# A four-layer cross-attention block on one core: another wait for v's copy, a term behind the relu, the relu in one pass with its bias folded into bf2

## The reference

```python
def _attention(x, src, dist, bias, ...):
    q = einsum('bfd,dnh->bfnh', x, Wq) * H ** (-0.5)
    k = einsum('btd,dnh->btnh', src, Wk);  v = einsum('btd,dnh->btnh', src, Wv)
    hbias = relu(dist[..., None] @ Wth + bth)          # 32 terms
    qs_bias = (hbias @ Wto + bto)[..., 0]
    w = softmax(einsum('btnh,bfnh->bnft', k, q) + bias + qs_bias[:, None])
    return einsum('bfnh,nhd->bfd', einsum('bnft,btnh->bfnh', w, v), Wo)

for i in range(4):
    x = x + _attention(_norm(x), ctx, dist, bias, Wq[i], Wk[i], Wv[i], Wo[i], ...)
    y = relu(_norm(x) @ Wf1[i] + bf1[i]) @ Wf2[i] + bf2[i]
    x = x + y
```

## Time and profile before

| | |
|---|---|
| median of 3 runs | 1341.23 us (1339.73 to 1343.92) |
| profiled execution | 1341.62 us, span 1339.6 us |
| TensorE matmul busy | 1208.2 us, 90% of the span |
| TensorE weight load | 991.7 us, 74% |
| VectorE | 1113.0 us, 83% |
| ScalarE | 1058.4 us, 79% |
| GpSimd | 719.8 us, 54% |
| DMA | 26.67 MB, 20 GB/s on average |

### The profile page before, as it was taken

The page is one execution under the profiler, slowest core; times in us unless marked ns, Lnnn a source line. Parts: engine busy times, 40 slices in busy tenths (PEclk is TensorE's granted clock), DMA queues, the critical chain, the costliest instruction groups (busy, mean ns, idle before and its releaser), DMA issues. The chain is left out here.

```text
span 1339.6 us, 36553 instructions
## 1 busy us (share of the span) xinstructions
PE 1208.2 (90%) x11184; PEld 991.7 (74%) x11184; DVE 1113.0 (83%) x4800; ACT 1058.4 (79%) x3353; POOL 719.8 (54%) x828
## 2 busy tenths in 40 slices
PE   2699999999999999999999999999999999789997
PEld 1577777777787777777777777877777777666665
DVE  4888888888888888888888888888888887579997
ACT  4688888888888888888888787878887865578896
POOL 3666666666666666656666665666666643211110
PEclk9899999999999999999999999999999999899999
DMA  6000000011100000011000000110000000000000
GB/s 189 17 1 17 2 18 1 17 33 34 35 17 2 17 2 17 2 57 43 10 9 10 10 2 18 49 43 9 18 1 25 2 2 4 1 10 14 14 16 9
DMA packets 32320, 26.67 MB, mean 20 GB/s; under 512 B 6648, under 2 KB 27008, under 8 KB 32128
## 3 DMA queue, kind: packets, MB, share of 16 engines
q1 hardware_dynamic: 32128, 24.35, 6.3%
HBM read 23.29 MB, written 1.05 MB: 18 GB/s over the span
## 5 line engine op out<-in xcount | busy, mean ns | idle before, releaser
L768 ACT ACTIVATE prob<-score,nmax 128x128 f32<-128x128 f32 x1024 | 397.1, 392 | 95.6 <-DVE nmax L963 93.9
L1367 POOL TENSOR_TENSOR prob<-prob,rinv 128x512 f32<-128x512 f32 x256 | 266.6, 1041 | 377.7 <-DVE rinv L971 377.0
L751 ACT ACTIVATE relu_z<-dist_g,cst_all 128x512 f32<-128x512 f32 x386 | 295.4, 805 | 12.5 <-DMA dist_g<-in_fside_BxSxS 10.1
L916 DVE SCALAR_TENSOR_TENSOR M<-relu_z,cst_all,M 128x512 f32<-128x512 f32 x370 | 277.7, 751 | 7.1 <-ACT relu_z L751 3.3
L963 DVE CUSTOM_DVE_ANT_0 score<-L,bias 128x128 f32<-128x128 f32 x1024 | 232.7, 283 | 2.0 <-PE L L485 0.9
L768 ACT ACTIVATION_READ_ACCUMULATOR prob<-score,nmax 128x1 f32 x1024 | 196.1, 191 | 0.0
L630 PEld LDWEIGHTS M<-wo,oT 128*128 128x128 f32 x1024 | 119.1, 191 | 66.7 <-ACT oT L780 66.6
L495 PE MATMUL T<-ident,prob 128*128 128x128 f32 x1024 | 161.3, 280 | 0.5 <-POOL prob L1367 0.5
L485 PE MATMUL L<-kT,qT 64*128 64x128 f32 x2048 | 149.7, 286 | 1.4 <-DVE nmax L963 1.4
L509 PE MATMUL O<-probT,v 128*64 128x128 f32 x2048 | 140.1, 278 | 8.8 <-issue 7.3
L630 PE MATMUL M<-wo,oT 128*128 128x128 f32 x1024 | 131.3, 281 | 15.0 <-ACT oT L780 15.0
(11 more groups left out here) (134 smaller groups left out, 2174.2 us busy)
## 6 DMA issues: line engine op xcount, KB each, us to landing
dist_g<-in_fside_BxSxS SPq DMA_DIRECT2D x16, 256.0 KB, 2.8
mask_g<-in_mask_Bx1x1xS_ff SPq DMA_DIRECT2D x16, 256.0 KB, 3.1
wk<-in_L_xattn_Wk SPq DMA_DIRECT2D x4, 512.0 KB, 3.5
wv<-in_L_xattn_Wv SPq DMA_DIRECT2D x4, 512.0 KB, 3.5
wq<-in_L_xattn_Wq SPq DMA_DIRECT2D x4, 512.0 KB, 3.9
wo<-in_L_xattn_Wo SPq DMA_DIRECT2D x4, 512.0 KB, 4.2
wf<-in_L_xattn_Wf SPq DMA_DIRECT2D x8, 256.0 KB, 2.8
xr<-in_x SPq DMA_DIRECT2D x16, 64.0 KB, 1.9
```

The costliest lines, as they stand in the source:

```text
L751: nc.scalar.activation(relu_z[:, z_slot(g, k), :], dist_g[:, :, :], ACT.Relu, bias=cst(g, C_BTH + k), scale=cst(g, C_WTH + k)).then_inc(z_ ...
L768: last = nc.scalar.activation(prob[:, c, m, :], score[:, c, m, :], ACT.Exp, bias=nmax[:, c, m:m + 1], scale=-1.0, accum_out=rsum[:, c, m:m ...
L916: vec.scalar_tensor_tensor(out=bias_acc[:, :], in0=relu_z[:, z_slot(g, k), :], scalar=weight, in1=bias_acc[:, :], op0=ALU.mult, op1=ALU.ad ...
L1367: gp.tensor_tensor(prob[:, c, :, :], prob[:, c, :, :], rinv[:, c, :].rearrange("p (m o) -> p m o", o=1).broadcast_to([P, 4, P]), ALU.mult) ...
```

## The change

Four edits, which share their semaphores.

1. ScalarE's copy of the first half of v waits for P V of octet 0 of the unit before last to be written (`after(g, i - 1, 2, 0)`), where it waited for octet 1 (`after(g, i - 1, 2, 1)`). The half that is overwritten is read by octet 0 alone.
2. On VectorE `terms(g, i, 0)` moves from ahead of the h2T copy to behind the relu.
3. The relu becomes one pass of 128x512: max(M1, -bf1) in place of max(M1 + bf1, 0). These differ by bf1, which is constant over positions.
4. The missing bf1 Wf2 is made once a layer and added to bf2: GpSimd writes -bf1 (128x4) and bf1 spread over 128 columns (128x512), TensorE multiplies it by Wf2 (four matmuls into T0), VectorE adds the result to bf2b. This is done in the first step for layer 0, and for the others in the second step of the last group of the layer before (GpSimd's part a step earlier). wf2, bf1c and bf2b get two buffers, and are loaded at the second group of the layer before.

```diff
+        def fold_layer(g, i):
+            if (g, i) == (0, 0):
+                return 0
+            if i == 1 and g % GROUPS_PER_LAYER == GROUPS_PER_LAYER - 1 and g < GROUPS - 1:
+                return g // GROUPS_PER_LAYER + 1
+            return None
@@ TensorE
+            def fold(g, i, l):
+                pe.wait_ge(w_f2, l * 16 + 16)
+                pe.wait_ge(fold_rep, 2 * l + 2)
+                pe.wait_ge(pT_even, after(g, i, 2, 0))
+                for c in range(FILT // P):
+                    last = mm(T[0][:, 0:P], bf1_rep[:, c, :], wf2[:, l % 2, c, :], start=c == 0, stop=c == FILT // P - 1)
+                last.then_inc(fold_done, 1)
...
+                folds = [] if i < 0 else [l for l in range(LAYERS) if (4 * g + i - 1) in ((0,) if l == 0 else (16 * l - 3,))]
+                for l in folds:
+                    pe.wait_ge(fold_kept, l + 1)
                 if prev:
                     turn(g, i - 1, 2)
...
                     queries(g, i + 1, 1)
+                if fold_layer(g, i) is not None:
+                    fold(g, i, fold_layer(g, i))
                 if cur:
                     apply(g, i, 0)
@@ ScalarE
                     act.wait_ge(v_done, after(g, i + 1, 2, 0))
-                    wait(act, pv_done, after(g, i - 1, 2, 1))
+                    wait(act, pv_done, after(g, i - 1, 2, 0))
@@ VectorE
                     inverse(g, i - 1, 3)
-                if i < GROUP:
-                    terms(g, i, 0)
...
-                    for c in range(FILT // P):
...
-                        last = vec.tensor_scalar(hid[:, i % 2, c, :], M1[:, c * P:(c + 1) * P], bf1c[:, c:c + 1], 0.0, ALU.add, ALU.max)
-                    last.then_inc(hid_kept, 1)
...
+                    vec.tensor_tensor(hid[:, i % 2, :, :], M1[:, :].rearrange("p (c t) -> p c t", c=FILT // P),
+                                      nbf1[:, l % 2, :].rearrange("p (c o) -> p c o", o=1).broadcast_to([P, FILT // P, P]),
+                                      ALU.max).then_inc(hid_kept, 1)
+                if i < GROUP:
+                    terms(g, i, 0)
...
+                if fold_layer(g, i) is not None:
+                    l = fold_layer(g, i)
+                    dve.wait_ge(fold_done, l + 1)
+                    dve.wait_ge(w_b2, l * 16 + 16)
+                    vec.tensor_tensor(bf2b[:, l % 2, :], T[0][:, 0:P], bf2b[:, l % 2, :], ALU.add).then_inc(fold_kept, 1)
@@ GpSimd
+                if fold_layer(g, i + 1) is not None:
+                    l = fold_layer(g, i + 1)
+                    pool.wait_ge(w_b1, l * 16 + 16)
+                    wait(pool, hid_kept, BATCHES * (l - 1))
+                    gp.tensor_scalar(nbf1[:, l % 2, :], bf1c[:, l % 2, :], -1.0, None, ALU.mult).then_inc(fold_rep, 1)
+                    wait(pool, fold_done, l)
+                    gp.tensor_copy(bf1_rep[:, :, :], bf1c[:, l % 2, :].rearrange("p (c o) -> p c o", o=1).broadcast_to(
+                        [P, FILT // P, P])).then_inc(fold_rep, 1)
                 if prev or there(g, i + 2):
                     root_pair(g, i)
```

More of the change, by code:

```diff
@@ L149, in block_program @@
         wf1 = sb("wf1", [P, FILT])
-        wf2 = sb("wf2", [P, FILT // P, P])
-        bf1c = sb("bf1c", [P, FILT // P])
-        bf2b = sb("bf2b", [P, P])
+        wf2 = sb("wf2", [P, 2, FILT // P, P])
+        bf1c = sb("bf1c", [P, 2, FILT // P])
+        nbf1 = sb("nbf1", [P, 2, FILT // P])
+        bf1_rep = sb("bf1_rep", [P, FILT // P, P])
+        bf2b = sb("bf2b", [P, 2, P])
         dist_g = sb("dist_g", [P, GROUP, P])
@@ L252, in block_program @@
         f1_done, hid_kept, f2_done = sem("f1_done"), sem("hid_kept"), sem("f2_done")
+        fold_rep, fold_done, fold_kept = [sem("fold_" + n) for n in ("rep", "done", "kept")]
         f_consts, f_in, f_gate_in, tanh_done = sem("f_consts"), sem("f_in"), sem("f_gate_in"), sem("tanh_done")
@@ L350, in load_f2 @@
             def load_f2(l):
-                sp.dma_start(wf2[:, :, :], Wf2[bass.ds(l, 1), :, :].rearrange("l (c p) d -> p (l c) d", p=P)).then_inc(w_f2, 16)
+                sp.dma_start(wf2[:, l % 2, :, :], Wf2[bass.ds(l, 1), :, :].rearrange("l (c p) d -> p (l c) d", p=P)).then_inc(w_f2, 16)
             def load_b1(l):
-                sp.dma_start(bf1c[:, :], bf1[bass.ds(l, 1), :].rearrange("l (c p) -> p (l c)", p=P), allow_slow_non_contiguous=True).then_inc(w_b1, 16)
+                sp.dma_start(bf1c[:, l % 2, :], bf1[bass.ds(l, 1), :].rearrange("l (c p) -> p (l c)", p=P), allow_slow_non_contiguous=True).then_inc(w_b1, 16)
             def load_b2(l):
-                sp.dma_start(bf2b[:, :], bf2[bass.ds(l, 1), :].broadcast_to([P, P])).then_inc(w_b2, 16)
+                sp.dma_start(bf2b[:, l % 2, :], bf2[bass.ds(l, 1), :].broadcast_to([P, P])).then_inc(w_b2, 16)
             for w, col in ((Wth.rearrange("l o k -> o l k"), C_WTH), (bth.rearrange("(o l) k -> o l k", o=1), C_BTH),
@@ L399, in group @@
                             load_o(l)
-                            wait_first(sp, consts, xb_done, after(g, -1, 1))
-                            load_b2(l)
                         if i == 1:
@@ L404, in group @@
                             load_f1(l)
[L405 to L408, removed]
+                    if gg == 1 and l < LAYERS - 1 and i == 0:
+                        k = g - 1
+                        wait_first(sp, consts, xb_done, after(k, -1, 1))
+                        load_b2(l + 1)
+                        wait_first(sp, consts, hid_kept, after(k, -1, 1))
+                        load_b1(l + 1)
+                        wait_first(sp, consts, f2_done, after(k, -1, 1), fold_done, l + 1)
+                        load_f2(l + 1)
                     if isinstance(gg, int) and gg == GROUPS_PER_LAYER - 1 and not last and i == 2:
@@ L606, in step @@
                     for c in range(FILT // P):
-                        last = mm(T[0][:, 0:P], hid[:, i % 2, c, :], wf2[:, c, :], start=c == 0, stop=c == FILT // P - 1)
+                        last = mm(T[0][:, 0:P], hid[:, i % 2, c, :], wf2[:, layer_of(g, i - 2) % 2, c, :], start=c == 0, stop=c == FILT // P - 1)
                     last.then_inc(f2_done, 1)
@@ L1032, in step @@
                 if old:
-                    for c in range(FILT // P):
[L1035 to L1039, removed]
-                        last = vec.tensor_scalar(hid[:, i % 2, c, :], M1[:, c * P:(c + 1) * P], bf1c[:, c:c + 1], 0.0, ALU.add, ALU.max)
-                    last.then_inc(hid_kept, 1)
+                    dve.wait_ge(f1_done, after(g, i - 2, 1))
+                    wait(dve, f2_done, after(g, i - 4, 1))
+                    l = layer_of(g, i - 2)
+                    if i % GROUP == 2:
+                        dve.wait_ge(fold_rep, 2 * l + 1)
+                    vec.tensor_tensor(hid[:, i % 2, :, :], M1[:, :].rearrange("p (c t) -> p c t", c=FILT // P),
[3 more added lines that the diff above has]
+                    terms(g, i, 0)
                 if prev:
@@ L1435, in step @@
                     if i % GROUP == 1:
-                        pool.wait_ge(w_b2, layer_of(g, i - 1) * 16 + 16)
-                    gp.tensor_tensor(xb[:, (i - 1) % 2, :], x_of(g, i - 1), bf2b[:, :], ALU.add).then_inc(xb_done, 1)
+                        pool.wait_ge(fold_kept, layer_of(g, i - 1) + 1)
+                    gp.tensor_tensor(xb[:, (i - 1) % 2, :], x_of(g, i - 1), bf2b[:, layer_of(g, i - 1) % 2, :], ALU.add).then_inc(xb_done, 1)
                 if early:
```

## The result

The changed kernel takes 1271.30 us (median of 4 runs, 1271.12 to 1271.44); its time is 0.9479 of that of the kernel before (95% interval 0.9462 to 0.9496), whose median of 4 runs is 1340.58. The forecast was 1275, the range 1257 to 1300. The profiled execution took 1271.33 us, span 1269.5.

A forecast was written before the change was run, and what follows sets the result against it. A loop of waits through ScalarE's v copy was taken to hold TensorE at 17.36 us a step. Steps of 16.14 save 72.0, plus 1.5 behind them, less 5.5 and 1.4: 1341.6 - 66.6 = 1275 us, range 1257 to 1300.

The forecast's parts named there:

- the loop: Waits over ScalarE, VectorE and TensorE; after the edit T0, probT copy, reciprocal, h2T copy, F1, next T0: 15.93 us.
- The loop's terms: T0 to probT copy 0.77, to reciprocal 3.57, to h2T copy 4.81, to F1 0.34, to next T0 6.44 us.
- The mis-sized term on VectorE: Stretch from reciprocal to h2T copy: 5.47 us falls to 4.81 once the 0.66 bias term moves behind the relu.
- without this edit it would be 16.59: Step time in us if the bias term stayed ahead of the h2T copy, in place of 15.93.
- F2 late by 0.06: TensorE's F2 waits for hT: could start 3.40 us after F1 against 3.34 bare, in three steps of four.
- The fourth step: One step in four, with no term to move but the bias sum (0.65 counted) on VectorE: 16.58 us.
- The folds: Making bf1 Wf2 once a layer: 1.5 us each for three layers, 1 for the first in the ramp; 5.5 lost.
- the 1.4 of late steps: Allowance of 1.4 us off the gain, for steps in the mean that were late for causes that stay.
- The floor: TensorE's step if it never waits, 15.75 us; rival that it binds, steps of 15.8: 1254 us, 10 in 100.
- The relu that costs as much as four passes: Rival: VectorE's one-pass relu takes up to 1.04 us, F2 0.4 late on average: about 1300 us, 21 in 100.
- the slower pass: Rival: VectorE's relu pass between F1 and hT copy reaches 2.1 us, making the kernel slower: 1364 us, 3 in 100.
- the wait that isn't what holds ScalarE: Rival: the v copy would wait for the values group anyway, only term and relu gain: 1317 us, 4 in 100.

The follow-up runs named there:

- the four runs: Against the kernel before: v wait alone 1282.67 us; plus term moved, four passes 1288.40; v wait plus one pass, term ahead 1280.72; the changed kernel 1271.30.
- the first two runs: Kernel before with only the v copy's wait changed: 1282.67 us; changed kernel with only that wait turned back to octet 1: 1329.87 us.

## Why the prediction was right, point by point

- **The v wait** was the largest part, and the loop goes on through the turned quad: right. Shown by the v wait alone (4.4% of 5.2) and by the wait of the probT copy that took its place (40.9 us in 63 steps).
- **The loop's terms.** T0 to probT copy: 0.77 forecast, 656.35 - 655.66 = 0.69 measured. probT copy to reciprocal: 3.57 and 643.92 - 640.34 = 3.58. Reciprocal to F1: 4.81 + 0.34 = 5.15 and 649.00 - 643.92 = 5.08. F1 to T0: 6.44 + 0.06 = 6.50 and 655.66 - 649.00 = 6.66. Sum: 15.99 and 16.01. The terms are off by up to 0.16 and the sum by 0.02, so part of its exactness is luck.
- **The mis-sized term on VectorE.** Reciprocal to h2T copy was put at 5.47 - 0.66 = 4.81 and is 4.59. The one step I read had h and h2 0.18 longer than others. The kernel before, VectorE, that step and a later one:

```profile
618.09 0.78 DVE L999 TENSOR_SCALAR h<-x_all,mv,rs 128x128 f32<-128x128 f32 x2
...
670.26 0.60 DVE L999 TENSOR_SCALAR h<-x_all,mv,rs 128x128 f32<-128x128 f32 x2
```

  With the smaller differences at T0 and F1 that is also why "without this edit it would be 16.59" was too high: with one pass and the term in its old place it is 16.30. I should have read three steps. In its place another path binds: h starts at 647.25, the transpose of h2 0.40 later, scores and F1 follow bare. F1 doesn't wait for h2T in an ordinary step at all.
- **F2 late by 0.06**: the mechanism was right, the size was not. Values to F2 is 1.06 for 0.86, so 0.20 late. The hT copy to F2 is 0.43 where I took the 0.34 of another pair, and bare values take 0.86, not 0.90: the step I took as bare already had a little of this wait. That the move and the one pass need each other is shown by the four runs; the forecast's 0.50 with four passes is 0.63.
- **The fourth step**: 16.58 forecast, 16.37 measured. Here the loop is the forecast's own, through the h2T copy (632.94): 0.69 + 3.58 + 5.39 + 0.31 + 6.40 = 16.37, for 0.77 + 3.57 + 5.46 + 0.34 + 6.44. The bias sum makes the stretch from reciprocal to h2T copy 0.80 longer, not 0.65; the step is only 0.36 longer than the others since in those the h2T copy had 0.18 to spare and F2 was 0.26 late, and both are used up.
- **The relu pass**: 692 ns, the same as L952; taken from the right row. The rule on hopping sources (the Trainium skill, Vector Engine (DVE) Microarchitecture Reference, Measured stream behaviour on trn2) would have made it an estimated 0.3 us longer; the trace shows nothing of it, so the rule doesn't reach this column that is read over and over.
- **The folds** were put at 5.5 us. The step with TensorE's part costs 0.87, as forecast (0.9). GpSimd's part costs 0.1, not 0.6: its copy takes 609 ns, below my lower bound of 0.77, and most of it and of the tiny pass lies in the 0.59 us for which GpSimd stood idle ahead of sd, which starts 0.13 later than in other steps. Three times 0.97 is 2.9. The first fold can't be told from the ramp's scatter: the first Wo comes 0.40 later than before, and stands between 73.5 and 75.3 in the other kernels with folds, between 73.5 and 74.9 in those without. The granted clock in the ramp differs too, 0.83 on average from 40 to 80 us against 0.87 before.
- **Sum.** 66.6 forecast, 70.1 measured in the span. With the three folds and the 1.4 of late steps the forecast's mean step is 16.24, measured 16.19: that is 2.9 of the 3.5, and 0.6 is the ramp. The stretch behind the steps gave 1.45 for a forecast of 1.5, and that is luck: the steps in it gave 3.25, and the longer time at the lower clock, for which the forecast had no term, took 1.80 back. From kernel to kernel the part behind the 64th Wo varies from 179.1 to 186.8 us.
- **The rivals.** The floor doesn't bind: it is 15.53, the sum of the bare distances from group to group in this trace, not 15.75 (Wo and the values group ahead of it are 0.11 and 0.04 shorter than I took them, and the like); with the term behind hT two steps near the end took 15.55 and 15.56. The relu that costs as much as four passes, the slower pass and the wait that isn't what holds ScalarE are out by the relu's 692 ns and the first two runs. The clock stayed at its higher level (2.4 GHz) in the steps, as before, from 80 us to 1080 us; that the change had no effect on it holds for that stretch only.

## What to carry to other kernels

When a wait sits on a loop over several engines, add up the loop as it will close after the edit, term by term; the gain is the old loop less the new one or the floor, not the wait's own length. An instruction moved off one path lands in front of another consumer: look what that one waits for, and put it behind that too, if nobody is late by it (here another 0.7 to 1.2%). But ask first what it covers: a term that hid GpSimd's latency could be moved only at a loss of 2.6%.

## What the runs showed of the hardware

- A TensorE group that had to wait takes a little more than its wait: P V begins 1.05 after an F2 that waited and 0.98 after one that didn't; the turn begins 1.89 after a Wo that waited and 1.78 after one that didn't. 0.07 to 0.11 us each; the same values return in the other kernels wherever these groups wait.
- On VectorE a tiny scaling pass took 0.43 us behind a wait for GpSimd, and 0.16 where GpSimd had been done before.
- At the lower clock level the four fp32 matmuls of F2 took 2.00 us until the next group started (1104.83 to 1106.83), at the higher one 1.09 (1176.74 to 1177.83). How long the lower level lasted behind the steps differed from kernel to kernel, with no order in it that these runs show.
- GpSimd copies 128x512 from a column read over and over in 609 ns, its tensor_scalar pass over a full tile takes 767.
